# A mixture-of-experts block around attention: expert numbers read sixteen tiles at a time, and three accumulators in place of two

## The reference

```python
x = x + 0.5 * ffn(layernorm(x), ...)
x = x + attention(layernorm(x), ...)
x = x + 0.5 * ffn(layernorm(x), ...)      # the same weights again
```

```python
shared = silu_and_mul(x @ shared_gate_up_w.T) @ shared_down_w.T * sigmoid(x @ sgate_w.T)
topk_w, topk_ids = top_k(softmax(x @ gate_w.T), 4)          # 16 experts, 4 of them for each token
for e in range(16):
    coef = sum(where(topk_ids == e, topk_w, 0), axis=-1)
    acc += (silu_and_mul(x @ w13[e].T) @ w2[e].T) * coef[:, None]   # 256 -> 2 x 176 -> 256
out = shared + acc
```

## Time and profile before

| | us |
|---|---|
| median of 3 runs | 709.12 |
| the runs | 709.12, 709.79, 703.31 |
| profiled execution: its time | 704.64 |
| profiled execution: its span | 702.9 |

### The profile page before, as it was taken

How to read it: one execution, slowest core, us unless ns; L and a number is a source line. 1 busy time by engine, 2 the same in 40 slices (tenths; PEclk the granted TensorE clock), 3 DMA queues, 4 the chain that set the end, 5 groups by cost and what they waited for, 6 DMA issues and landing times.

```text
span 702.9 us, 14497 instructions
## 1 busy us (share of the span) xinstructions
PE 577.8 (82%) x4310; PEld 297.5 (42%) x4310; DVE 496.1 (71%) x1414; ACT 413.4 (59%) x830; POOL 241.8 (34%) x197
## 2 busy tenths in 40 slices
PE   4896578888870788999989999999989968889880
PEld 2453346555540344333322223333355645656550
DVE  6698866755555768888898888887476646666563
ACT  6477466655440567675837776768773335656540
POOL 3477136778762100000000000000027736766662
PEclk9999599999995699999999999999989989999995
DMA  5399946765765011101000000000004545777667
GB/s 174 126 305 346 303 128 116 124 113 94 117 88 135 0 35 35 35 1 35 1 2 1 1 1 1 1 1 1 1 1 151 188 135 90 123 124 124 114 94 201
DMA packets 56234, 64.37 MB, mean 92 GB/s; under 512 B 5729, under 2 KB 50273, under 8 KB 56162
## 3 DMA queue, kind: packets, MB, share of 16 engines
q0 software_dynamic: 16608, 21.77, 18.8%
q1 hardware_dynamic: 33040, 31.60, 14.9%
q10 hardware_dynamic: 6514, 10.10, 4.7%
HBM read 31.05 MB, written 32.39 MB: 90 GB/s over the span
## 4 chain that ended last, share of the span: by engine, by line
PE 43%; DMA 23%; DVE 10%; issue 9%; POOL 6%; ACT 5%; SPq 1%; ACTq 0%; POOLq 0%; DVEq 0%
DMA acc_dram<-R 15%; PE psum L1530 10%; PE psum L1500 9%; PE psum L1288 8%; POOL xg_dram L681 5%; PE psum L1513 5%; DMA R<-xg_dram 3%; PE psum L1496 3%; DVE m_part L1239 2%; PE psum L1517 2%; DVE W_ex L1046 2%; DMA acc_dram<-R,vals 1%; DMA R<-acc_dram 1%; DMA kT<-w_dram 1%; ACT W_ex L723 1%
## 5 line engine op out<-in xcount | busy, mean ns | idle before, releaser
L1239 DVE TENSOR_REDUCE m_part<-psum 128x1 f32<-128x512 f32 (+3 forms) x304 | 182.5, 657 | 30.8 <-PE psum L1500 29.2
L868 ACT ACTIVATE R<-psum 128x1024 f32<-128x1024 f32 x144 | 141.0, 1022 | 43.3 <-PE psum L1513 33.1
L692 POOL DMA_INDIRECT acc_dram<-R x88 | 138.1, 1569 | 66.7 <-DMA acc_dram<-R 29.1
L1288 PE MATMUL psum<-W_ex,R 128*128 x564 | 104.0, 322 | 2.3 <-ACT R L782 2.3
L708 POOL TENSOR_TENSOR R<-R 128x256 f16<-128x256 f32 x6 | 4.0, 693 | 280.3 <-ACT R L850 280.3
L1500 PE MATMUL psum<-kT,qTs 128*128 128x512 f16 (+3 forms) x384 | 98.7, 331 | 1.9 <-DVE m_part L1239 1.2
L681 POOL DMA_INDIRECT xg_dram<-R,o_tok x64 | 71.0, 1109 | 46.9 <-DVE o_tok L1007 28.0
L1530 PE MATMUL psum<-R,vals 128*32 128x512 f32 x576 | 76.7, 604 | 0.4 <-ACT oT L876 0.2
L782 ACT ACTIVATE R<-psum 128x512 f16<-128x512 f16 x94 | 55.6, 594 | 36.2 <-PE psum L1336 33.8
L1077 DVE SCALAR_TENSOR_TENSOR R<-psum,R 128x176 f32<-128x176 f32 x94 | 32.1, 341 | 57.2 <-ACT R L789 57.1
L1288 PE MATMUL psum<-xT,W_sh 128*128 128x512 f16 x264 | 64.1, 395 | 6.0 <-DVE R L1057 3.1
(11 more groups left out here) (190 smaller groups left out, 953.2 us busy)
## 6 DMA issues: line engine op xcount, KB each, us to landing
R<-xg_dram SPq DMA_DIRECT2D x88, 144.0 KB, 2.4
kT<-w_dram ACTq DMA_DIRECT2D x15, 512.0 KB, 5.9
xg_dram<-pad_sb SPq DMA_DIRECT2D x33, 144.0 KB
R<-acc_dram SPq DMA_DIRECT2D x16, 256.0 KB, 4.5
acc_dram<-rot_b SPq DMA_DIRECT2D x2, 1152.0 KB, 9.0
acc_dram<-ex SPq DMA_DIRECT2D x4, 576.0 KB, 3.4
kT<-w_dram SPq DMA_DIRECT2D x4, 384.0 KB, 4.2
acc_dram<-R POOLq DMA_INDIRECT x88
```

What stands on the lines that cost most here:

```text
L692: nc.gpsimd.indirect_dma_start(acc_dram[f][n % 2], bass.IndirectOffsetOnAxis(ap=tile_rows(n, I32)[:, D + NE:D + NE + 1], axis=0), y_sb[:, ...
L868: nc.scalar.activation(prob[:, n % 2, 2 * pair:2 * pair + 2, :].rearrange("p g n -> p (g n)"), psum[:, 1024 * pair:1024 * (pair + 1)], ACT ...
L1239: nc.vector.tensor_reduce(m_part[:, h:h + heads, kt // 4], ps, axis=AX.X, op=ALU.max).then_inc(free_of(e), 1)
L1288: ins = nc.tensor.matmul(o, stat(a, k), mov(b, k), start=first and n == 0, stop=last and n == 3 * k_parts - 1, **kw)
```

## The change

It has two parts. **Reads in a row:** TensorE reads `tab_e` no more once in each turn but sixteen entries in a row, in turns -1, 15 and 31 (15 entries in the last), at the place where the single read stood; the other turns read nothing. **Three accumulators:** `NA = 3`; tile `n` adds to accumulator `n % 3` and waits for the add of tile `n - 3`. Each add in block 0 waits for the clearing of its own accumulator. The end of a block loads three sums (the first into `xn`, which is free by then, and without waiting for the last product), and VectorE adds three.

```diff
+NA = 3
...
         def adds_up_to(n):
-            return 16 * (n // 2 + 1)
+            return 16 * (n // NA + 1)
...
                 if n >= 8:
                     sp.wait_ge(s_xgp, n - 7)
-                    sp.wait_ge(s_add[n % 2], adds_up_to(n - 8))
+                    sp.wait_ge(s_add[(n - 8) % NA], adds_up_to(n - 8))
...
             def load_sums(f):
                 last = f * NX + NX - 1
-                sp.wait_ge(s_ye, last + 1)
-                for i, n in enumerate((last - 1, last)):
-                    sp.wait_ge(s_add[n % 2], adds_up_to(n))
+                for i, n in enumerate((last - 2, last - 1, last)):
+                    if i == 1:
+                        sp.wait_ge(s_ye, last + 1)
+                    sp.wait_ge(s_add[n % NA], adds_up_to(n))
...
-                    if f == 0 and s in (3, 4):
+                    if f == 0 and 3 <= s < 3 + NA:
                         clear_first(s - 3)
...
-                if n >= 2:
-                    pool.wait_ge(s_add[n % 2], adds_up_to(n - 2))
+                if n >= NA:
+                    pool.wait_ge(s_add[n % NA], adds_up_to(n - NA))
                 nc.gpsimd.indirect_dma_start(
-                    acc_dram[f][n % 2], bass.IndirectOffsetOnAxis(ap=tile_rows(n, I32)[:, D + NE:D + NE + 1], axis=0),
-                    y_sb[:, n % 4, :], None, compute_op=ALU.add).then_inc(s_add[n % 2], 16)
+                    acc_dram[f][n % NA], bass.IndirectOffsetOnAxis(ap=tile_rows(n, I32)[:, D + NE:D + NE + 1], axis=0),
+                    y_sb[:, n % 4, :], None, compute_op=ALU.add).then_inc(s_add[n % NA], 16)
...
-                for g in range(NP):
-                    add_first(f, g)
+                for i in range(NA - 1):
+                    for g in range(NP):
+                        add_sums(f, i, g)
...
                     if 0 <= s < NX:
                         expert_gate_up(f, s, expert[s])
-                    if s + 1 < NX:
-                        expert[s + 1] = pe.value_load(tab_e[0:1, s + 1:s + 2], min_val=0, max_val=NE - 1)
+                    if (s + 1) % 16 == 0:
+                        for i in range(s + 1, min(s + 1 + 16, NX)):
+                            expert[i] = pe.value_load(tab_e[0:1, i:i + 1], min_val=0, max_val=NE - 1)
```

More of the change, by code:

```diff
@@ L247, in build @@
         xg_dram = nc.dram_tensor("xg_dram", (NE * CAP + P, XR), F32).ap()
-        acc_dram = [[nc.dram_tensor(f"acc_dram{f}{a}", (T + P, D), F32).ap() for a in range(2)] for f in range(2)]
+        acc_dram = [[nc.dram_tensor(f"acc_dram{f}{a}", (T + P, D), F32).ap() for a in range(NA)] for f in range(2)]
         x_res = sb("x_res", [P, TT, D], F32)
@@ L300, in build @@
         acc = R2[:, :].rearrange("p (a t d) -> p a t d", a=2, t=TT)
+        sums = [xn, acc[:, 0], acc[:, 1]]
         prob = R1[:, 0:4096].rearrange("p (s g n) -> p s g n", s=2, g=GLO)
@@ L384, in build @@
         s_tab_p = sem("s_tab_p")
-        s_zero = [sem(f"s_zero{f}") for f in range(2)]
+        s_zero = [sem(f"s_zero{a}") for a in range(NA)]
+        s_zero_second = sem("s_zero_second")
         s_token = sem("s_token")
@@ L408, in build @@
         s_ysb = sem("s_ysb")
-        s_add = [sem(f"s_add{i}") for i in range(2)]
-        s_acc_first = [sem(f"s_acc_first{g}") for g in range(NP)]
-        s_acc = [sem(f"s_acc{g}") for g in range(NP)]
+        s_add = [sem(f"s_add{a}") for a in range(NA)]
+        s_acc = [[sem(f"s_acc{i}_{g}") for g in range(NP)] for i in range(NA)]
         s_zero_src = sem("s_zero_src")
@@ L569, in clear_first @@
                 sp.dma_start(acc_dram[0][a].rearrange("(t p) d -> p t d", p=P),
-                             zeros.unsqueeze(1).to_broadcast([P, TT + 1, D])).then_inc(s_zero[0], 16)
+                             zeros.unsqueeze(1).to_broadcast([P, TT + 1, D])).then_inc(s_zero[a], 16)
             def clear_second(i):
@@ L576, in clear_second @@
                 sp.dma_start(acc_dram[1][a][:, half].rearrange("(t p) d -> p t d", p=P),
-                             zeros2.unsqueeze(1).to_broadcast([P, TT + 1, P])).then_inc(s_zero[1], 16)
+                             zeros2.unsqueeze(1).to_broadcast([P, TT + 1, P])).then_inc(s_zero_second, 16)
             def load_sums(f):
                 last = f * NX + NX - 1
-                sp.wait_ge(s_ye, last + 1)
-                for i, n in enumerate((last - 1, last)):
-                    sp.wait_ge(s_add[n % 2], adds_up_to(n))
+                for i, n in enumerate((last - 2, last - 1, last)):
+                    if i == 1:
+                        sp.wait_ge(s_ye, last + 1)
+                    sp.wait_ge(s_add[n % NA], adds_up_to(n))
                     for g in range(NP):
-                        rows = acc_dram[f][n % 2][g * 2 * P:(g + 1) * 2 * P, :].rearrange("(t p) d -> p t d", p=P)
-                        sp.dma_start(acc[:, i, 2 * g:2 * g + 2, :], rows).then_inc((s_acc_first, s_acc)[i][g], 16)
+                        rows = acc_dram[f][n % NA][g * 2 * P:(g + 1) * 2 * P, :].rearrange("(t p) d -> p t d", p=P)
+                        sp.dma_start(sums[i][:, 2 * g:2 * g + 2, :], rows).then_inc(s_acc[i][g], 16)
             xv = x_in.rearrange("(t p) d -> t p d", p=P)
@@ L606, in _ @@
                     sp.wait_ge(s_zero_src, 1)
-                    for i in range(4):
+                    for i in range(2 * NA):
                         clear_second(i)
@@ L687, in add_up @@
                 pool.wait_ge(s_ysb, n + 1)
-                if s == 0:
-                    pool.wait_ge(s_zero[f], 64 if f else 32)
-                if n >= 2:
-                    pool.wait_ge(s_add[n % 2], adds_up_to(n - 2))
+                if f == 0 and s < NA:
+                    pool.wait_ge(s_zero[s], 16)
+                if f == 1 and s == 0:
+                    pool.wait_ge(s_zero_second, 16 * 2 * NA)
+                if n >= NA:
+                    pool.wait_ge(s_add[n % NA], adds_up_to(n - NA))
                 nc.gpsimd.indirect_dma_start(
-                    acc_dram[f][n % 2], bass.IndirectOffsetOnAxis(ap=tile_rows(n, I32)[:, D + NE:D + NE + 1], axis=0),
-                    y_sb[:, n % 4, :], None, compute_op=ALU.add).then_inc(s_add[n % 2], 16)
+                    acc_dram[f][n % NA], bass.IndirectOffsetOnAxis(ap=tile_rows(n, I32)[:, D + NE:D + NE + 1], axis=0),
+                    y_sb[:, n % 4, :], None, compute_op=ALU.add).then_inc(s_add[n % NA], 16)
             constants()
@@ L801, in ffn @@
                 if f:
-                    act.wait_ge(s_zero[1], 64)
+                    act.wait_ge(s_zero_second, 16 * 2 * NA)
                 nc.scalar.activation(ex[:], lg[:], ACT.Exp).then_inc(s_ex, 1)
@@ L1102, in result_out, with add_sums @@
                 if n >= 4:
-                    dve.wait_ge(s_add[n % 2], adds_up_to(n - 4))
+                    dve.wait_ge(s_add[(n - 4) % NA], adds_up_to(n - 4))
                 nc.vector.tensor_scalar(y_sb[:, n % 4, :], y_bank[n % 2][:, 0:D], coef[:, n % 4:n % 4 + 1], None,
                                         ALU.mult).then_inc(s_ysb, 1)
-            def add_first(f, g):
+            def add_sums(f, i, g):
                 pair = slice(2 * g, 2 * g + 2)
-                dve.wait_ge(s_acc_first[g], 16 * (f + 1))
-                link(nc.vector.tensor_tensor(x_res[:, pair, :], x_res[:, pair, :], acc[:, 0, pair, :], ALU.add))
+                dve.wait_ge(s_acc[i][g], 16 * (f + 1))
+                link(nc.vector.tensor_tensor(x_res[:, pair, :], x_res[:, pair, :], sums[i][:, pair, :], ALU.add))
             def combine(f, g):
                 pair = slice(2 * g, 2 * g + 2)
-                dve.wait_ge(s_acc[g], 16 * (f + 1))
-                nc.vector.tensor_tensor(x_res[:, pair, :], x_res[:, pair, :], acc[:, 1, pair, :],
+                dve.wait_ge(s_acc[NA - 1][g], 16 * (f + 1))
+                nc.vector.tensor_tensor(x_res[:, pair, :], x_res[:, pair, :], sums[NA - 1][:, pair, :],
                                         ALU.add).then_inc(s_comb, 1)
```

## The result

| | before | changed |
|---|---|---|
| median, us | 707.86 (4 runs, 703.31 to 709.79) | **759.66** (4 runs, 753.52 to 761.82) |
| ratio | | 1.074, 95% interval 1.069 to 1.079 |
| span of the profiled execution | 702.9 | 751.6 |
| mean granted clock | 0.936 | 0.902 |

The change makes the kernel slower by 52 us. The direction was forecast, the size was not: +25.3 us were forecast for the profiled execution, and its span grew by 48.7. The median, forecast at 732, lies above the range of 706 to 752.

What follows compares the result with a forecast made beforehand. Two accumulators held turns to 2.25 to 2.4 us, row buffers next at 2.15. Block 1 +12.6, block 0 +12.7, ends nothing: 704.6 + 25.3 = 729.9, plus half of 4.5 gave 732 us, range 706 to 752.

Steps and rivals of the forecast that it cites:

- stops: TensorE, turns -1, 15 and 31 of each block: sixteen reads in a row take 9.6 us, fifteen 9.0.
- accumulators: GpSimd's adds in the expert parts: a third accumulator ends their wait, bringing at most 0.2 us a tile.
- Bound: Expert parts: adds into the accumulators hold 15% of the span; two accumulators allow 2.25 to 2.4 us a tile.
- the three stops a block: Sign in TensorE's timeline: gaps of 9 to 10 us at turns -1, 15 and 31, clock halved behind them.
- A read in a row costs 0.6 us: TensorE's sequencer: load 0.30, sum 0.15 and gaps make 0.6 us a read, without overlap.
- The rival in which reads overlap: TensorE's rows of reads: sixteen take only 3.2 us, so 690 us, faster; chance 0.16.
- The start of block 0: Reads before block 0: first two slow, 11.5 us in all, tile 3 at 98.3 against 90.86, +7.4.
- What is late next are the row buffers, 2.15.: Eight row buffers, expert parts: the loop of add and load takes 10.75 us for five tiles, 2.15 a tile.
- more adds in flight land later: Expert parts: adds of 4.8 and loads of 3.2 us make the loop 12.5, so 754 us; chance 0.14.
- The ends, net nothing: Each block's end: last add about 2 us sooner, against +2 for four more loads and sums; net nothing.

Runs made afterwards that it cites:

- e14: The changed kernel with each row of sixteen reads made one load into sixteen registers, without bounds checks; 708.05 us against 711.8 before, ratio 0.995.
- e6: The changed kernel timed again, beside the kernel before on one chip; 762.31 us, ratio 1.072 to the kernel before.
- e5: The kernel before, unchanged, timed and traced again on another chip; 711.21 us (one run).
- e4: The changed kernel with each of the sixteen reads of turn 15 issued twice; 836.57 us, ratio 1.106 to the kernel before.
- e13: The kernel before with three accumulators only, single reads kept, in the fourth group; median 710.95 us against 711.8, ratio 0.988.
- e8: The changed kernel with row numbers copied out, so a row buffer's next load no longer waits for its add; 728.27 us, ratio 1.020 to the kernel before.
- e15: The changed kernel with one load for sixteen values, unchecked, and row numbers copied out to free row buffers before their add; 675.00 us against 711.8, ratio 0.951.
- e1: The kernel before with three accumulators only, single reads kept, in the first group; 758.57 us against 757.01, ratio 1.000.

## Why the prediction was right and wrong

3 to 46 and the starts, in us; "stops" is the change against e14, "accumulators" is e14 against before:

| | forecast | measured |
|---|---|---|
| stops: start of block 0 | 7.4 | 12.0 |
| stops: block 0, 3 to 46 | 19.2 | 16.9 |
| stops: start of block 1 | 3.2 | 4.6 |
| stops: block 1, 3 to 46 | 19.2 | 14.1 |
| stops together | 49.0 | 47.6 |
| accumulators: block 0, 3 to 46 | -13.9 | -1.8 |
| accumulators: block 1, 3 to 46 | -9.8 | +4.0 |
| together | +25.3 | +49.8 |

(The forecast's sum isn't divided like this; the column is that sum, with 43 turns at 2.15 us, 92.5, for what the accumulators leave without stops, and 4.1 more in block 0. The traces compared are from different chips. With e6 in place of the change the stops come to 47.0. The kernel before takes 109.5 and 104.7 in e5, so -1.8 and +4.0 are hardly more than two traces of one kernel differ by.)

- **Bound, direction, the three stops a block: right.** Gaps at turns -1, 15 and 31, the clock halved behind them, GpSimd hardly waiting for adds (11 times, 4.3 us, where never was forecast): each is in the rows above.
- **A read in a row costs 0.6 us: nearly right**, 0.66 measured (the change, e4). The load (0.30), the sum (0.15) and the assertion (0.02) are 0.47 of it, the rest are gaps between them. The rival in which reads overlap is dead. The Trainium skill's "Runtime: NRT & Kernel Launch", section "Instruction fetch mechanics", gives about 200 ns a register even in bulk. The traces have another figure in both cases: 0.30 us for the load alone where sixteen instructions stand in a row, and some 0.09 for each register where one instruction loads sixteen (1.31 to 1.58 us in block 1 of e14). The Trainium skill's floor of about 600 ns for such a load, in "DMA: Bandwidth & Descriptors", section "Latency and other measured facts", isn't a floor here: the load took 0.30, and only the whole read with its check and gaps comes near it, at 0.66. The remedy that it names, unrolling, is what the change does by sixteen, and no run shows that it lowers the price of a read.
- **The start of block 0: too small**, 12.0 instead of 7.4. Two slow reads were taken from the earlier trace rows, which show three reads and no more. Seven were slow, 0.8 to 1.45 us for the load alone, starts 1.1 to 1.8 us apart from 82.9 to 92.7, while the weights' DMA was busy.
- **The step that failed: "What is late next are the row buffers, 2.15."** It was right about what is late next and wrong about its length: 2.47 us a tile over the whole stretch of block 1 (106.1 us for 43 turns in e13, 106.3 in e14; 92.5 forecast). By that term the forecast was off: -23.7 forecast, +2.2 measured. These 25.9 us, less the 1.4 by which the stops came out smaller, are the 24.5 that the sum missed.
  - The loop of the earlier trace rows was there with 11.34 us. It was shortened to 10.75 by putting the median load of all 88, 2.4 us, in the place of its own 3.22. The loop of e13 has the same parts: 3.75 us to the add (3.68 in rows 7), 3.98 for it (3.8 forecast), 0.83 to the load (0.79), 3.32 for the load. Other loads in the chains took 3.31 and 3.46 in e13 and 3.54, 3.44 and 4.72 in e14. Not all are so long: 2.46 once in e13, and 2.55 in the change's loop above, where the add was long instead.
  - That explains only part. With 11.34 left as it was, the term would have been 97.5 us a block, still 9 short of the 106.3 measured. The whole stretch goes at 12.3 us for five tiles in e13, 11.9 in the kernel before. Which part of the loop holds this rest was not separated.
  - So the accumulators and the buffers were limits of nearly equal height, and taking the one away brought nothing that the time clearly shows.
  - On the same stretches the stops were forecast 7 us too large (38.4 against 31.1). A likely reason is that with the longer loop more of each stop falls where TensorE would have waited for rows anyway: with the loop open, e8 against e15, they cost 35.4. That was not tried by itself.
- **The rival "more adds in flight land later"** came nearest: 754 us, like the other rivals' sums on the scale of the profiled execution, which took 753.5. Its loops of 12.5 are nearly the size of those measured, its reason fits only in part. The adds in the chains took 3.7 to 4.8 us; before, too, they took 3.3 to 4.8. What grew more clearly is the load, median of the block-1 stretch 2.3 us before, 2.5 in e13 and 3.1 in e14. That adds cause this by contention was not tried by itself.
- **The ends, net nothing: right.** From tile 46 of block 1 to the end it takes 25.2 us, before 25.3. What was gained and what was paid in it, 2 us each in the forecast, was not measured singly.

## What to carry to other kernels

Work gathered in a row to pay for it once is only cheaper if the row itself is: look for the dependent instruction behind each member, ask what had hidden the single ones, and then ask whether one instruction can do the row (here 1.4 us instead of 10.7). Before a wait is removed, measure the closed loops beside it by two of their own rows, start to start, and don't replace a member by a median over the whole program; where two loops stand within a few per cent of each other, as here, opening one may bring nothing until the other is opened too.

## What was not expected of the hardware

- The kernel before takes 708 to 712 us on some chips and 757 on others (there once 738), and the difference lies outside the expert parts. Of one and the same kernel, e1 (757 us chip) has its first transposes at 107.3 us, e13 at 84.3; from tile 46 of block 0 to the first transposes of block 1 it takes 397.1 us in e1, 366.3 in e13; 3 to 46 is 112.1 and 106.5 against 111.2 and 106.1. Up to the first transposes the DMA engines move 196 GB/s in e1 and 251 in e13, and the granted clock is 0.81 against 0.91. What stalls there was not looked into further.
- With the loop open, loads of rows get longer without any harm: their median over the whole span is 2.4 us in the kernel before and 3.0 in e15.
- One load into sixteen registers took 3.92 us in front of block 0, under the weights' DMA, and 1.31 to 1.58 in block 1 of e14, 1.10 to 1.86 in block 1 of e15.
